# Attention layer with routed experts on one core: the second quad of values and the expert ranks at other places, and half of the causal mask on GpSimd

## What is computed

```python
q, k, v = jnp.split(target @ w_qkv, 3, axis=-1)          # 16 heads of 8 channels
scores = jnp.einsum('bhqd,bhkd->bhqk', q, k) * (1.0 / np.sqrt(HD))
causal = (jnp.arange(t)[:, None] >= jnp.arange(t)[None, :]).astype(scores.dtype)
scores = scores * causal - (1.0 - causal) * NEG
attn = jax.nn.softmax(scores, axis=-1)
out = jnp.einsum('bhqk,bhkd->bhqd', attn, v)
...
x = _layernorm(x + _L0_attn_ref(x, ...))                 # attention, its norm, a second norm
x = _layernorm(x + _L0_ffn_ref(x, ...))                  # top 2 of 14 experts, weighted
```

## Time and profile before

| | before |
|---|---|
| median of 3 runs | 470.4 us (468.29 to 470.57) |
| the profiled execution, its time | 471.32 us |
| the profiled execution, its span | 469.6 us |
| PE busy over the span | 364.5 us (78%) |
| DVE busy | 317.6 us (68%) |
| ACT busy | 276.6 us (59%) |
| POOL busy | 254.9 us (54%) |
| mean granted clock of PE | 0.931 of full speed |

### The profile page before, as it was taken

One profiled execution on the slowest core, in us unless ns is written; L12 is line 12 of the kernel. 1 busy time (PEld: TensorE's weight loads), 2 busy tenths in 40 slices (PEclk: granted clock), 3 DMA queues, 4 the chain that ended last, 5 costly groups with the idle time before them and its releaser, 6 DMA issues. The chain is left out here.

```text
span 469.6 us, 13082 instructions
## 1 busy us (share of the span) xinstructions
PE 364.5 (78%) x4355; PEld 268.6 (57%) x4355; DVE 317.6 (68%) x1001; ACT 276.6 (59%) x672; POOL 254.9 (54%) x341
## 2 busy tenths in 40 slices
PE   3648999887898989898889786307999888984940
PEld 2325566555566656665556454207988877871940
DVE  7355568978588898889888854354777666750591
ACT  2203666666477667767776485206999888840074
POOL 5600043545346654665455467641777777774382
PEclk9999999999799999999999899556999999998895
DMA  3521247864323323333230010033333333311742
GB/s 100 151 62 48 61 117 192 228 134 104 88 72 106 93 77 87 98 92 91 63 84 25 25 43 30 23 108 74 103 97 103 99 94 101 98 47 54 249 147 89
DMA packets 72254, 44.09 MB, mean 94 GB/s; under 512 B 12641, under 2 KB 67955, under 8 KB 72076
## 3 DMA queue, kind: packets, MB, share of 16 engines
q1 hardware_dynamic: 64856, 32.70, 26.5%
q0 software_dynamic: 4672, 9.36, 6.0%
q10 hardware_dynamic: 2660, 1.20, 1.0%
HBM read 18.61 MB, written 12.43 MB: 66 GB/s over the span
## 5 line engine op out<-in xcount | busy, mean ns | idle before, releaser
L909 DVE TENSOR_REDUCE row_max<-M 128x4 f32<-128x1024 f32 (+1 forms) x96 | 117.1, 1219 | 35.0 <-PE M L1192 34.2
L705 ACT ACTIVATE probs<-S 128x768 f32<-128x768 f32 x128 | 102.6, 817 | 52.9 <-PE S L1159 51.1
L670 POOL DMA_INDIRECT results<-tile_rows x78 | 79.9, 1024 | 35.7 <-issue 20.9
L635 POOL DMA_INDIRECT sorted_rows<-x,row_no x64 | 65.0, 1015 | 41.2 <-DVE row_no L967 27.9
L1097 DVE COPY probs<-experts 128x642 f32 x78 | 47.8, 613 | 24.8 <-DVE tile_rows L1106 22.5
L1186 PE MATMUL M<-k_stack,q_stack 64*128 64x128 bf16 (+1 forms) x512 | 40.8, 262 | 29.9 <-DVE row_max L909 28.9
L1375 PE MATMUL M<-probs,hT 128*128 128x128 f32 x312 | 52.1, 291 | 9.0 <-DVE tile_rows L1106 5.8
L1210 PE MATMUL O<-probs,diag 128*32 128x256 f32 (+1 forms) x1024 | 56.6, 341 | 0.5 <-DVE row_chosen L948 0.5
L792 ACT ACTIVATE hT<-S,probs 128x128 f32<-128x128 f32 x156 | 49.0, 364 | 2.5 <-PE S L1368 1.4
L1375 PEld LDWEIGHTS M<-probs,hT 128*128 128x128 f32 x312 | 41.4, 194 | 15.9 <-ACT hT L792 8.0
L1368 PE MATMUL S<-rows_t,probs 128*128 128x128 f32 x312 | 49.6, 283 | 0.3 <-ACT rows_t L786 0.3
(11 more groups left out here) (193 smaller groups left out, 709.2 us busy)
## 6 DMA issues: line engine op xcount, KB each, us to landing
q_stack<-diag SPq DMA_DIRECT2D x96, 64.0 KB
tile_rows<-sorted_rows SPq DMA_DIRECT2D x78, 64.5 KB, 1.9
k_stack<-diag SPq DMA_DIRECT2D x78, 64.0 KB
xin<-in_L_attn_target_dram SPq DMA_DIRECT2D x16, 128.0 KB, 2.5
xres<-in_L_attn_target_dram SPq DMA_DIRECT2D x16, 128.0 KB, 2.5
q_stack<-results SPq DMA_DIRECT2D x8, 256.0 KB, 3.1
k_stack<-results SPq DMA_DIRECT2D x8, 256.0 KB, 3.7
out_dram<-probs SPq DMA_DIRECT2D x8, 256.0 KB, 2.3
```

Source lines behind the costliest of these rows:

```text
L635: pool.indirect_dma_start(sorted_rows, bass.IndirectOffsetOnAxis(ap=row_no[:, q * 2 * TT + n:q * 2 * TT + n + 1], axis=0), x2[:, q, n % 2, ...
L670: pool.indirect_dma_start(results, bass.IndirectOffsetOnAxis(ap=y_rows[:, slot, D:ROW].bitcast(U32), axis=0), y_rows[:, slot, 0:D], None, ...
L705: act.activation(probs[:, n].rearrange("p (a q) -> p a q", a=2), S[n % 2][:, :].rearrange("p (a q) -> p a q", a=2)[:, :, 0:T + P], ACT.Exp ...
L909: dve.tensor_reduce(row_max[:, (r - 2) % R, :, g0:g0 + ng, half], M_both[:, :].rearrange("p (a h k) -> p a h k", a=2, h=ng), X, ALU.max).t ...
```

## The change

Four edits, all in phase one. The second quad of values of sequence t-3 leaves u = 7 and is computed at u = 0 of the next body, behind that body's first unit of maxima; ACT's copy of O moves with it. The ranks on PE go from ahead of the second unit of maxima to behind it (the turn of x stays ahead of it), and DVE reads them after its second reduction, while the first half of the norm (`yg`) goes ahead of that reduction. Score units 3 to 6 of each sequence no longer get the four mask matmuls; POOL sets the masked places of `probs` to zero after the exponential, with two `affine_select` instructions of 256 elements per partition for each unit, and `values` waits for them (semaphore `masked`).

```diff
@@ -277,6 +277,7 @@
         shift_copied = sem("shift_copied")
         s_ready = sem("s_ready")
         exp_done = sem("exp_done")
+        masked = sem("masked")
         pv_done = sem("pv_done")
         o_copied = sem("o_copied")
         o_turned = sem("o_turned")
@@ -387,13 +388,16 @@
         NM = len(M_UNITS)
         assert NP == 8
+        SELECTED = (3, 4, 5, 6)
         def s_unit(t, u):
             return (t - 3, u - 2) if u >= 2 else (t - 4, u + NP - 2)
         def pv_quad(t, u):
-            return {2: (t - 4, 2), 3: (t - 4, 3), 5: (t - 3, 0), 7: (t - 3, 1)}.get(u)
+            return {0: (t - 4, 1), 2: (t - 4, 2), 3: (t - 4, 3), 5: (t - 3, 0)}.get(u)
         def stack_count(t):
@@ -614,6 +618,15 @@
                         pool.tensor_tensor(rstd2[:, :], var_eps2[:, :], minus_half[:, 0:TT], ALU.pow).then_inc(rstd2_done, 1)
                         pool.wait_ge(rstd2_done, t - 4)
                         pool.tensor_tensor(centre2[:, :], neg_mean2[:, :], rstd2[:, :], ALU.mult).then_inc(centred2, 1)
+                    s, n = s_unit(t, u)
+                    if on(s) and n in SELECTED:
+                        pool.wait_ge(exp_done, NP * s + n + 1)
+                        for at in (0, T):
+                            diag = probs[:, n, :].rearrange("p (a q) -> p a q", a=2)[:, :, at:at + P]
+                            last = pool.affine_select(out=diag, in_=diag, compare_op=ALU.is_ge, fill=0.0, base=0,
+                                                      pattern=[[0, 2], [1, P]], channel_multiplier=-1)
+                        last.then_inc(masked, 1)
                     if u == 6 and on(t - 4):
                         after(pool, ys_done, t - 4)
                         pool.tensor_tensor(x_beta[:, :, :], xres[:, r], beta_all[:, None, :].broadcast_to([P, TT, D]),
@@ -705,6 +718,11 @@
                         act.activation(probs[:, n].rearrange("p (a q) -> p a q", a=2),
                                        S[n % 2][:, :].rearrange("p (a q) -> p a q", a=2)[:, :, 0:T + P], ACT.Exp,
                                        scale=SCALE).then_inc(exp_done, 1)
+                    if u == 0 and on(t - 4):
+                        act.wait_ge(pv_done, 4 * (t - 4) + 2)
+                        after(act, o_turned, 2 * (t - 4))
+                        act.copy(heads_t[:, 0:2], O[:, :].rearrange("p (k q) -> p k q", k=2)).then_inc(o_copied, 1)
                     if u == 1 and on(t) and not early(t):
                         act.wait_ge(xT_ready, t + 1)
                         act.copy(xT[:, r], G[:, 0:T]).then_inc(xT_copied, 1)
@@ -767,11 +785,6 @@
                         act.wait_ge(x2_done, t - 4)
                         act.copy(x2[:, (r - 5) % R, 1, :, 0:D], x2[:, (r - 5) % R, 0, :, 0:D]).then_inc(x2_twice, 1)
                         act.copy(x2_all[:, t - 5].rearrange("p (i d) -> p i d", i=TT), x2[:, (r - 5) % R, 0, :, 0:D]).then_inc(x2_kept, 1)
-                    if u == 7 and on(t - 3):
-                        act.wait_ge(pv_done, 4 * (t - 3) + 2)
-                        after(act, o_turned, 2 * (t - 3))
-                        act.copy(heads_t[:, 0:2], O[:, :].rearrange("p (k q) -> p k q", k=2)).then_inc(o_copied, 1)
             run(act, body)
@@ -943,6 +956,12 @@
                     wait_apart(dve, stats_done, (2 * TT) * (t - 5) + TT)
                     for i in range(TT):
                         dve.bn_aggr(moments[:, i], stats[:, i]).then_inc(stats_done, 1)
+                if on(t - 5):
+                    dve.wait_ge(stats_done, 2 * TT * (t - 4))
+                    for i in range(TT):
+                        dve.scalar_tensor_tensor(out=yg[:, i], in0=y[:, i], scalar=moments[:, i, 0:1], in1=gamma_all[:, :],
+                                                 op0=ALU.subtract, op1=ALU.mult).then_inc(yg_done, 1)
+                reduce(1)
                 if on(t - 6):
                     dve.wait_ge(rank_ready, t - 5)
                     dve.tensor_tensor(row_chosen[:, :, :, :], chosen[:, :, :, :],
@@ -954,12 +973,6 @@
                         if t == B + 5:
                             dve.tensor_reduce(seen_wide[:, :, :], both[:, q].rearrange("p k e -> p e k")[:, :, None, :].broadcast_to(
                                 [P, E, PIECES, TT + 1]), X, ALU.add).then_inc(seen_widened, 1)
-                reduce(1)
-                if on(t - 5):
-                    dve.wait_ge(stats_done, 2 * TT * (t - 4))
-                    for i in range(TT):
-                        dve.scalar_tensor_tensor(out=yg[:, i], in0=y[:, i], scalar=moments[:, i, 0:1], in1=gamma_all[:, :],
-                                                 op0=ALU.subtract, op1=ALU.mult).then_inc(yg_done, 1)
                 if on(t - 6):
                     dve.wait_ge(rank_read, t - 5)
                     n = (r - 6) % R
@@ -1152,12 +1165,14 @@
                         rows = slice(TILE * a, TILE * a + TILE)
                         last = pe.matmul(S[n % 2][:, 512 * a + at:512 * a + at + nq], k_stack[rows, b, n, half * P:half * P + P],
                                          q_stack[rows, b, n, T - nq:T], start=(half == 0), stop=True, skip_group_check=True)
-                for c in range(2):
-                    for a in range(2):
-                        rows = slice(TILE * a, TILE * a + TILE)
-                        diag = S[n % 2][:, 512 * a:512 * a + 2 * T].rearrange("p (k q) -> p k q", k=2)[:, :, TILE * c:TILE * c + TILE]
-                        last = pe.matmul(diag, mask_s[rows, c], ident_fold[rows, None, :].broadcast_to([TILE, 2, TILE]), start=False,
-                                         stop=True, skip_group_check=True)
+                if n not in SELECTED:
+                    for c in range(2):
+                        for a in range(2):
+                            rows = slice(TILE * a, TILE * a + TILE)
+                            diag = S[n % 2][:, 512 * a:512 * a + 2 * T].rearrange("p (k q) -> p k q", k=2)[:, :, TILE * c:TILE * c + TILE]
+                            last = pe.matmul(diag, mask_s[rows, c], ident_fold[rows, None, :].broadcast_to([TILE, 2, TILE]), start=False,
+                                             stop=True, skip_group_check=True)
                 last.then_inc(s_ready, 1)
             def maxima(t, r, i):
@@ -1194,6 +1209,7 @@
                 last.then_inc(m_ready, 1)
             def values(t, r, s, k):
+                after(pe, masked, len(SELECTED) * s + len([n for n in SELECTED if n <= 2 * k + 1]))
                 pe.wait_ge(exp_done, NP * s + 2 * k + 2)
                 if k == 0:
                     pe.wait_ge(v_copied, s + 1)
@@ -1260,6 +1276,10 @@
                             pe.transpose(M[0][:, 0:E], gate_raw[:, :], ident[0:E, 0:E]).then_inc(gate_turned, 1)
                     if u == 2 and on(t) and not early(t):
                         project(t, r)
+                    if u == 1 and on(t) and not early(t):
+                        turn_x(t, r, lap)
+                    if u < NM and on(t - 2):
+                        maxima(t, r, u)
                     if u == 1 and on(t - 6):
@@ -1278,10 +1298,6 @@
                                       start=False, stop=False, skip_group_check=True)
                         pe.matmul(rank, earlier[:, :], both[:, q, 0:TT], start=False, stop=True,
                                   skip_group_check=True).then_inc(rank_ready, 1)
-                    if u == 1 and on(t) and not early(t):
-                        turn_x(t, r, lap)
-                    if u < NM and on(t - 2):
-                        maxima(t, r, u)
                     if u == 4 and on(t - 4):
                         pe.wait_ge(o_copied, 2 * (t - 3))
```

## The result

The changed kernel takes 472.24 us (median of 9 runs, 470.46 to 473.75) and the kernel before, on the same chip, 470.23 us (9 runs, 468.26 to 470.57). The ratio is 1.0052 with a 95% interval of 1.0029 to 1.0075: slower, by about 2.4 us. The two profiled executions stand the other way round (changed 470.65, before 471.32), since each is one draw out of a spread of 2 to 3 us. So where time went is read body by body, and what an edit is worth in all from the ratios.

What follows compares the result with a forecast made beforehand. No engine was taken as full: PE and DVE hand maxima and reductions to each other. Terms -0.4 - 1.0 - 0.8 + 9.0 + 1.5 - 0.7 = +7.6 gave 478.0 us against the median of 470.4; range 468.5 to 485.

Steps and rivals of the forecast that it cites:

- Hold of `chosen` and `both`: DVE ahead of the first reduction: POOL's mask 4 and `x_beta` hold these two-operand instructions, +0.75 in twelve bodies, +9.0.
- Its lower bound: The hold's low case: `chosen` and `both` are each caught by an `affine_select` only, 0.4 a body.
- Second quad: Values moved behind the first unit of maxima: that unit comes 0.79 earlier, DVE wins only its wait of 0.22.
- Mask of unit 4: PE ahead of the turn of x2 and the logits DVE waits for: four mask matmuls fewer gain 0.11 a body.
- Ranks: PE between second and third units of maxima, without slack: 0.11 of work plus two tiling switches, +0.29 a body.
- Last bodies: Bodies 18 and 19, chain through POOL: four mask units (3.4) against 1.66 idle ahead of the first norm, +1.5.
- Start: Three starts of bodies ahead of the ranks gain 0.33 each, together -1.0.
- Stall of body 8: Score unit 0 waits 3.38 for the shift's DMA; what body 8 loses ahead of it is absorbed, -0.7.
- Bodies 16 and 17: They have no projection, so the ranks find idle PE: -0.4 each, -0.8 together.
- PE alone setting the pace: Rival: reductions follow PE, about -0.5 in each of 15 bodies, time 464.5, reaching from 462 to 468; chance 0.12.
- No hold: Rival: `chosen` and `both` run unhindered beside POOL's work, sum -0.7, time about 470, no change; chance 0.20.
- The shift meeting the fourth scatter: Rival: DVE's shift is held by POOL's fourth scatter, 0.7 later, +8.4 over 12 bodies, 486; chance 0.10.

Runs made afterwards that it cites:

- e5: The changed kernel with `x_beta` put ahead of the mask of unit 4 on POOL; 469.25 us, ratio 0.9978 to the kernel before.
- e6: The changed kernel with no unit masked on POOL, so the two moves alone; 468.10 us, ratio 0.9963 to the kernel before.
- e18: The changed kernel with the ranks directly ahead of the projection, behind score unit 0; 471.31 us, ratio 1.0058 to the kernel before.
- e8: The changed kernel with `x_beta` first, ranks at the projection and the last two sequences masked by TensorE; 466.20 us, ratio 0.9916 to before.
- e7: The changed kernel with the last two sequences masked by TensorE in all units; 471.75 us, ratio 1.0049 to the kernel before.
- e17: The kernel before with only the masks of score units 3 to 6 given to POOL, nothing moved; 469.99 us, ratio 1.0035.

## Why the prediction was right or wrong

It forecast 478.0 and +7.6; the change costs 2.4 us. The direction and the cause were right, the size was not. The step that failed is the first term. By its own terms:

- **Hold of `chosen` and `both`**, +0.75 in each of 12 bodies (+9.0): the step that failed, in its size. `x_beta` does hold `both`, and that is the largest cost (e5), but it is 0.46, and 0.49 on the path (y to R0 is 1.55, and 1.06 with the masks on TensorE, e6). It also stands in eleven of the twelve bodies, not in body 6. The plan of POOL was good: from y on, mask 4 was to end at 0.49 and `x_beta` at 1.19, and they end at 0.43 and 1.12. What went wrong is the addition behind it. It put the whole 0.72 of `x_beta` behind the end of `chosen` (211.25), as if POOL too had waited, where `x_beta` starts as soon as mask 4 is over and 0.16 of it was past by then. The release comes 0.10 behind POOL's end, not 0.14, and the selects are 0.07 shorter: 0.16 + 0.04 + 0.07 = 0.27 of the 0.29. Its lower bound, 0.4 for a hold by a mask only, was too high as well: e5 has 0.11.
- **Second quad, -0.22**: -0.32 (e6, y to R0). The recorded wait of 0.22 understated by 0.1 what is won when it goes.
- **Mask of unit 4, -0.11**: right, R2 to y 10.29 to 10.18.
- **Ranks, +0.29**: +0.22, of which 0.13 goes away at the projection (e18, e8) and 0.09 stays. The 0.09 is not the ranks': it lies between R0 and R1, where DVE with `yg` now works through 1.92 without a wait, and had waited 0.24 for PE within 1.83 before. That `yg` could cost there was not in the sum; no run moves `yg` alone.
- **Per middle body** the four terms made +0.71, and measured +0.28: 0.26 of the difference is the hold, 0.10 the quad, 0.07 ranks and `yg`.
- **Last bodies, +1.5**: +2.1, and e7 confirms the cause in the bodies. The term read only body 19; each of the two lost 1.1.
- **Start, -1.0**: body 5 does go from 15.53 to 15.15 (15.14 in e7 and e18), as forecast. The first y also comes 1.0 earlier (64.51, before 65.51), but that is not shown to be the change's: it comes at 63.43 in e18 and 64.55 in e7, which both are the changed kernel up to there.
- **Stall of body 8, -0.7**: -1.1 between these two executions. The wait is 3.05 in e7, which is the changed kernel up to that place, so this size is not shown either.
- **Bodies 16 and 17, -0.8**, so +0.7 with the hold: body 16 goes from 15.00 to 15.15, and 17 can't be compared, since the clock was low in it before.

Put together place by place (body 7 of before without the 0.87 of a wait for a DMA in it, body 17 compared with body 16 of before):

| place | forecast | the two traces |
|---|---|---|
| start, to y of body 6 | -1.0 | -1.4 |
| bodies 6 to 15, less the stall | +6.4 | +1.3 |
| bodies 16 and 17 | +0.7 | +0.3 |
| bodies 18 and 19 | +1.5 | +2.1 |
| sum | +7.6 | +2.4 |

The second row is nearly the whole of the 5.2 by which the sum was too high: 3.0 of it in the seven bodies 7, 9 and 11 to 15, 0.9 in body 6, 1.1 in body 8 and its stall. That the right column meets the ratio's +2.4 to the tenth is luck, since start and stall differ by about 1 us between executions, and so does what lies behind body 19.

Of the rivals, PE alone setting the pace is out: with the masks off PE and nothing moved (e17) a body got 0.05 longer. No hold is out by the 0.65, though that rival's time was the nearer one. The shift meeting the fourth scatter did not come: it went ahead of it, and gained 0.39 (0.63 to 0.24), of which the small copy took 0.16 and a longer wait for the logits 0.11 (1.11, before 1.00), so that it gave little, as the prediction said of that case. I had expected 16.1 a body and 0.9 of `both`; 15.72 and 0.65 are the same two statements with the mis-sized term. And that the time fell inside my range of 468.5 to 485 does not bear out the term: its case began at 474.

## What to carry to other kernels

A GpSimd instruction that is moved or made late cost here not where it was put, but where `x_beta`, 0.73 us long, came to run beside a VectorE instruction with two SBUF operands. List those on the critical stretch and put the long GpSimd read elsewhere, ahead of an instruction that reads PSUM, as `x_beta` beside y in e5. Count a wait as won or as cover, not both: two edits that each looked harmless (-0.08, +0.05 a body) cost 0.28 together. And small matmuls of another tiling belong beside a neighbour of their own kind: in this place that was worth 0.13 a body.

## What the runs showed of the hardware

- `affine_select` of 256 float32 elements in 128 partitions takes 0.41 on POOL, the same as 256 of bf16, and it holds a two-operand VectorE instruction for what is left of it: `both` 0.30 instead of 0.19 (e5), `chosen` 0.35 instead of 0.21 (body 6 of the changed kernel).
- A 32-element VectorE instruction took 0.63 beside an indirect DMA of POOL's and 0.24 ahead of it.
- The same kernel took 470 us in some series and 525 in others, with idle time at VectorE that no instruction released; kernels with half of the causal mask on POOL, and 256 matmuls fewer, lost about 40 us there, not 55. Not explained.
